# Output rows of a recurrent state-space layer with a mixture of experts: 32 indirect scatters from GpSimd in place of eight plain stores from SyncE

## The chip, the cores and the metric

The kernel runs on one core of one Trainium2 chip. The metric is the time of one execution on the device in microseconds (us). The core has five engines that run their own instruction streams and meet through semaphores: TensorE (PE in the profile, its weight loads PEld), VectorE (DVE), ScalarE (ACT), GpSimd (POOL) and SyncE (SP), which here only issues transfers. Sixteen DMA engines move the data between the memory of the chip and the on-chip tiles.

## The reference

The input x is 8 x 512 x 128 in float32: eight batches of 512 rows. With two branches s and g on the normalised rows, the output has x's shape and type:

```python
xn = _layernorm(x)
s = state_space(xn)        # conv over 3 rows, gates, a scan over the 512 rows of a batch, then
                           # ssm = ys @ D_w.T + D_b;  return ssm * gate
g = silu(mixture(xn))      # a dense gelu branch and 8 experts, 2 chosen per row
return x + s * g
```

In the scan each step is `s = layernorm(state @ A_bar + b_t)` and the row of y is `c_t * s`. Only the last line and the store of the result matter for the change.

## The kernel before

The 4096 rows (batch times 512) lie on the chip so that partition p holds the 32 consecutive rows 32p to 32p + 31: the tile X has the shape 128 partitions x 32 rows x 128 columns. NS = 32 is the number of such columns of rows, SUB = 4 how many of them make a group, NB = 8 the number of groups, L = 32 the rows of a partition. The kernel and this text call group n batch n; it holds rows 4n to 4n + 3 of each partition.

There are three blocks one after the other, with a barrier of all engines between them.

The first (up to about 100 us) loads the weights on SyncE (function load, L203) and x on ScalarE's queue, normalises, convolves and prepares weights. GpSimd's part begins with constants: memsets and masks (L244 to L265), the iota of 128x256 numbers into iota_i (L266) and its cast into rank (L268). After that GpSimd waits for the small weights (L274). VectorE uses rank when it chooses the experts (L776).

The second is the scan, in five rounds over 32 steps, with the eight experts of each group worked off beside it. It ends with the factor (silu of the mixture times the gate) of each group in the tile gi.

The third block, written out by hand engine by engine, makes the output, and it is what the change touches:

- VectorE normalises the states (L1373, four parts), TensorE transposes them (L1401, sixteen), ScalarE applies scale and bias (L1418), VectorE multiplies by C (L1379).
- TensorE makes ssm of a batch: a matmul of the bias over 512 columns (L1407) and eight products of 128x128 (L1409), in one of four banks.
- VectorE multiplies the bank by the factor and by 0.25 into outb, which is a view of the tile gi (L1383), and counts the semaphore gated_ssm.
- The residual x is added in place: by GpSimd for even batches (L1394, semaphore even_rows), by VectorE for odd ones (L1388, odd_rows).
- SyncE stores each batch, a transfer of 256 KB (L1426), as soon as even_rows or odd_rows says so, and waits at the end for all eight.

The store and the loop of GpSimd in two quotations:

```python
for n in range(NB):
    sp.wait_ge(sem("odd_rows" if n % 2 else "even_rows"), n // 2 + 1)
    sp.dma_start(rows_out[:, n * SUB:(n + 1) * SUB, :], outb[:, n]).then_inc(sem("out_stored"), 16)
```

Here rows_out is the output with the rows of a partition as its second axis, so that the four rows of a partition in one store are 2 KB in one piece.

Of the kernel before, what the change touches and what calls it, by code (L numbers as in the profile page):

```python
# [5 lines left out]
ALU = mybir.AluOpType  # L6
# [6 lines left out]
P = 128  # L13
# [19 lines left out]
def build(nc, I, out):  # L33
# [5 lines left out]
    SUB = T // P  # L39
# [5 lines left out]
    with ExitStack() as ctx:  # L45
        sems = {}

        def sem(name):
            if name not in sems:
                sems[name] = ctx.enter_context(nc.semaphore(name))  # L50
            return sems[name]

        def sb(name, shape, dt=F32):
            return ctx.enter_context(nc.sbuf_tensor(name, shape, dt))
# [9 lines left out]
        center = sb("center", [S, S])  # L64
        iota_i = sb("iota_i", [P, NS * E], mybir.dt.int32)
        rank = sb("rank", [P, NS, E])
        eps_col = sb("eps_col", [P, 1])
        junk_col = sb("junk_col", [P, 1])
        cols = sb("cols", [P, 24])
# [129 lines left out]
        with nc.Block() as front:  # L199
            @front.sync  # L200
            def _(sp):
                def load(dst, src, name="weights_loaded"):
                    sp.dma_start(dst, src).then_inc(sem(name), 16)  # L203

                def as_col(name):
                    return I[name].rearrange("(p a) -> p a", a=1)

                load(gens, I["L0_ffn_gens"].rearrange("m p n -> p m n"), "expm_loaded")
                load(A_in, I["L0_attn_A"], "expm_loaded")
                load(dt_row, I["L0_attn_dt_A"], "expm_loaded")  # L210
                load(gate_w[:, :, :], I["L0_attn_gate_w"].rearrange("(j p) h -> p j h", p=P), "matrices_loaded")
                load(BC_w[:, 0, :], I["L0_attn_B_w"], "matrices_loaded")
                load(BC_w[:, 1, :], I["L0_attn_C_w"], "matrices_loaded")
                load(D_w[:, 0, :], I["L0_attn_D_w"], "matrices_loaded")
                load(D_w[:, 1, :], I["L0_attn_D_w"], "matrices_loaded")
                load(ew2[:, :, :, :], I["L0_ffn_ew2"].rearrange("e (k p) d -> p e k d", p=P), "ew2_loaded")
                load(col["ln_in_g"], as_col("L0_attn_ln_in_g"))
                load(col["ln_in_b"], as_col("L0_attn_ln_in_b"))
                load(col["conv_b"], as_col("L0_attn_conv_b"))
                load(conv_w, I["L0_attn_conv_w"].rearrange("h a k -> h (a k)"))  # L220
                load(col["gate_b_in"], I["L0_attn_gate_b"][P:2 * P].rearrange("(p a) -> p a", a=1))
                load(col["ln_gamma"], as_col("L0_ffn_ln_gamma"))
                load(col["ln_beta"], as_col("L0_ffn_ln_beta"))
                load(col["B_b"][0:S], as_col("L0_attn_B_b"))
                for half in (slice(0, S), slice(S, P)):
                    load(col["ln_st_g"][half], as_col("L0_attn_ln_st_g"))
                    load(col["ln_st_b"][half], as_col("L0_attn_ln_st_b"))
                    load(C_b_col[half], as_col("L0_attn_C_b"))
                load(eb2[:, :], I["L0_ffn_eb2"])
                load(eb1_rows[:, :], I["L0_ffn_eb1"].rearrange("e (k p) -> (e k) p", p=P))  # L230
                load(gc_w_row, I["L0_ffn_gc_w"].rearrange("p a -> a p"))
                load(mgb_row, I["L0_ffn_moe_gate_b"].rearrange("(a p) -> a p", a=1))
                load(gc_b_row, I["L0_ffn_gc_b"].rearrange("(a p) -> a p", a=1))
                for i in range(3):
                    load(bias_in[i:i + 1, 0, :], I["L0_ffn_abel_b"].rearrange("(a p) -> a p", a=1), "biases_loaded")
                    load(bias_in[i:i + 1, 1, :], I["L0_attn_D_b"].rearrange("(a p) -> a p", a=1), "biases_loaded")
                    load(bias_in[i:i + 1, 2, :], I["L0_attn_gate_b"][0:P].rearrange("(a p) -> a p", a=1), "biases_loaded")
                load(abel_in[:, :], I["L0_ffn_abel_w"], "small_loaded")
                load(router_w[:, :], I["L0_ffn_moe_gate_w"], "small_loaded")
                load(ew1_in[:, :, :], I["L0_ffn_ew1"].rearrange("e d f -> d e f"), "ew1_loaded")  # L240

            @front.gpsimd
            def _(pool):
# [19 lines left out]
                pool.wait_ge(sem("shift2_ones"), 1)  # L263
                pool.memset(shift2[:, 0:P:SEG], 0.0)
                pool.memset(shift2[:, 1:P:SEG], 0.0)  # L265
                pool.iota(iota_i[:, :], pattern=[[0, NS], [-1, E]], base=E, channel_multiplier=0).then_inc(sem("iota_ready"), 1)  # L266
                pool.wait_ge(sem("iota_ready"), 1)
                pool.tensor_copy(rank[:, :, :], iota_i[:, :].rearrange("p (s e) -> p s e", s=NS)).then_inc(sem("rank_ready"), 1)  # L268
# [1096 lines left out]
        with nc.Block() as block:  # L1365
            @block.vector
            def _(dve):

                H2 = L // 4
                for g in range(4):  # L1370
                    part = slice(g * H2, (g + 1) * H2)
                    r = Rho[:, g * H2 + 1:(g + 1) * H2 + 1]
                    dve.tensor_tensor(Wst[:, part, :], Wst[:, part, :], r.unsqueeze(2).broadcast_to([P, H2, S]), ALU.mult).then_inc(sem("normalised"), 1)  # L1373

                for g in range(4):
                    part = slice(g * 4, (g + 1) * 4)
                    dve.wait_ge(sem("state_affine"), g + 1)
                    cs = csT[:, part, :].rearrange("p (b m) n -> p b m n", m=2)
                    dve.tensor_tensor(cs, cs, CT[:, 2 * g:2 * g + 2], ALU.mult).then_inc(sem("csT"), 1)  # L1379
                for n in range(NB):  # L1380

                    dve.wait_ge(sem("ssm"), n + 1)
                    dve.scalar_tensor_tensor(out=outb[:, n], in0=banks[4 + n % 4][:, :].rearrange("p (s h) -> p s h", s=SUB), scalar=0.25,  # L1383
                                             in1=factor[:, (n + 1) * SUB:(n + 2) * SUB, :], op0=ALU.mult, op1=ALU.mult).then_inc(sem("gated_ssm"), 1)

                    if n % 2:
                        dve.wait_ge(sem("gated_ssm"), n + 1)
                        dve.tensor_tensor(outb[:, n], outb[:, n], X[:, n * SUB:(n + 1) * SUB, :], ALU.add).then_inc(sem("odd_rows"), 1)  # L1388

            @block.gpsimd  # L1390
            def _(pool):
                for n in range(0, NB, 2):
                    pool.wait_ge(sem("gated_ssm"), n + 1)
                    pool.tensor_tensor(outb[:, n], outb[:, n], X[:, n * SUB:(n + 1) * SUB, :], ALU.add).then_inc(sem("even_rows"), 1)  # L1394

            @block.tensor
            def _(pe):
                for g in range(4):
                    pe.wait_ge(sem("normalised"), g + 1)
                    for q in range(4 * g, 4 * g + 4):  # L1400
                        t = pe.transpose(banks[g][:, (q % 4) * P:(q % 4 + 1) * P], Wst[:, 2 * q:2 * q + 2, :].rearrange("p k n -> p (k n)"), ident[:, :])  # L1401
                    t.then_inc(sem("cs_T"), 1)
                for n in range(NB):
                    pe.wait_ge(sem("csT"), n // 2 + 1)
                    if n >= 4:
                        pe.wait_ge(sem("gated_ssm"), n - 3)
                    pe.matmul(banks[4 + n % 4][:, :], ones3[:, :], D_b3, start=True, stop=False)  # L1407
                    for s in range(SUB):
                        t = pe.matmul(banks[4 + n % 4][:, s * P:(s + 1) * P], csT[:, 2 * n + s // 2, :], D_wT[:, s % 2, :],  # L1409
                                      start=False, stop=(s == SUB - 1))  # L1410
                    t.then_inc(sem("ssm"), 1)

            @block.scalar
            def _(act):
                for g in range(4):
                    act.wait_ge(sem("cs_T"), g + 1)

                    act.activation(csT[:, g * 4:g * 4 + 4, :], banks[g][:, :].rearrange("p (k n) -> p k n", k=4), ACT.Identity,  # L1418
                                   scale=col["ln_st_g"], bias=col["ln_st_b"]).then_inc(sem("state_affine"), 1)

            @block.sync
            def _(sp):
                rows_out = out.rearrange("b (q k) h -> (b q) k h", k=L)
                for n in range(NB):
                    sp.wait_ge(sem("odd_rows" if n % 2 else "even_rows"), n // 2 + 1)
                    sp.dma_start(rows_out[:, n * SUB:(n + 1) * SUB, :], outb[:, n]).then_inc(sem("out_stored"), 16)  # L1426
                sp.wait_ge(sem("out_stored"), 16 * NB)

# [26 lines left out]
```

## Time and profile before

| | us |
|---|---|
| timed runs (two) | 544.72 and 546.92 |
| their median | 545.82 |
| the profiled execution | 543.42 |
| its span, first to last instruction | 541.6 |
| TensorE busy in it | 444.0 (82%) |
| VectorE busy | 377.2 (70%) |
| ScalarE busy | 250.1 (46%) |
| GpSimd busy | 209.2 (39%) |

The profile is of one execution. Its span is 1.8 us shorter than that execution's own time, since it counts from the first to the last instruction. Starts are in us from the start of the span, durations of one instruction in us or ns as marked. Issues of transfers are not counted as busy time of the engine that issues them; they stand under its queue (SPq for SyncE).

### The profile page before, as it was taken

What the parts mean: (1) busy time and instruction counts of PE and PEld (TensorE: products, weight loads), DVE (VectorE), ACT (ScalarE), POOL (GpSimd) and SP (SyncE); (2) the same over time, 40 slices, a digit from 0 to 9 for tenths busy, and PEclk for the clock granted to TensorE, in tenths of its full rate; (3) what the DMA queues carried; (4) which work ended last, traced back from release to release, by engine and by line L of the source; (5) the groups of instructions that cost most, each with busy time, mean ns of one, the idle gap of its engine ahead of it and who ended that gap; (6) DMA issues with size and microseconds to landing.
All of it is one profiled execution on the core that took longest, in us unless ns stands there. A gap on an engine that the chain in (4) does not pass through costs nothing. (4 is left out here: it accounts for less than half of the span.)

```text
span 541.6 us, 13237 instructions
## 1 busy us (share of the span) xinstructions
PE 444.0 (82%) x4780; PEld 343.0 (63%) x4780; DVE 377.2 (70%) x1471; ACT 250.1 (46%) x597; POOL 209.2 (39%) x201
## 2 busy tenths in 40 slices
PE   2866799799889888988898898689889889998247
PEld 1766748477656666676676676567766566776135
DVE  3878579377878587777768676667677576868445
ACT  0325922445455335554455546154645355554420
POOL 2266645012532253243325414332443143425443
PEclk9959959899999798999999999799999799999759
DMA  8200000000000000000000000000000000000004
GB/s 268 79 7 0 2 1 1 2 1 2 2 2 2 1 2 1 1 2 1 2 2 0 3 1 1 2 1 2 1 2 2 1 1 2 2 1 2 0 4 155
DMA packets 6483, 7.65 MB, mean 14 GB/s; under 512 B 2424, under 2 KB 4378, under 8 KB 6426
## 3 DMA queue, kind: packets, MB, share of 16 engines
q1 hardware_dynamic: 5850, 4.77, 2.8%
q10 hardware_dynamic: 576, 2.10, 1.1%
q8 instruction: 39, 0.64, 0.5%
q14 instruction: 18, 0.15, 0.1%
HBM read 4.76 MB, written 2.10 MB: 13 GB/s over the span
## 5 line engine op out<-in xcount | busy, mean ns | idle before, releaser
L1336 POOL TENSOR_TENSOR xpad<-xpad 128x512 f32<-128x512 f32 x64 | 82.8, 1294 | 243.0 <-ACT xpad L1248 187.3
L1157 PE MATMUL bank<-ew,hT 128*128 128x128 f32 x1024 | 143.5, 289 | 0.0
L1248 ACT ACTIVATE xpad<-bank,wd 128x128 f32<-128x128 f32 x256 | 73.1, 369 | 128.4 <-PE bank L1157 128.2
L1157 PEld LDWEIGHTS bank<-ew,hT 128*128 128x128 f32 x1024 | 124.8, 195 | 9.1 <-issue 0.7
L1240 ACT ACTIVATE hT<-bank,eb_col 128x512 f32<-128x512 f32 x128 | 81.2, 687 | 50.7 <-PE bank L194 50.7
L980 PE MATMUL bank<-Mrep,wT 32*32 32x64 f32 x2560 | 69.7, 223 | 36.4 <-DVE wT L886 35.8
L980 PEld LDWEIGHTS bank<-Mrep,wT 32*32 32x32 f32 x2560 | 45.0, 106 | 77.8 <-issue 72.4
L896 DVE SCALAR_TENSOR_TENSOR ring<-bank,Rho,Dv 128x64 f32<-128x64 f32 x124 | 35.2, 284 | 65.1 <-PE bank L980 61.5
L192 PE MATMUL bank<-xf,ew_high 128*128 128x512 f32 x128 | 61.6, 481 | 0.0
L194 PE MATMUL bank<-xf,ew_rest 128*128 128x512 f32 x128 | 52.2, 408 | 0.0
L193 PE MATMUL bank<-xf,ew_high 128*128 128x512 f32 x128 | 52.2, 408 | 0.0
L852 DVE SCALAR_TENSOR_TENSOR roots<-z_all 128x1 f32<-128x1 f32 x96 | 34.0, 354 | 3.3
L886 DVE STREAM_TRANSPOSE wT<-ring 128x64 f32<-128x64 f32 x124 | 30.0, 242 | 2.0
L876 DVE CUSTOM_DVE_ANT_0 sqj<-ring,guess 128x64 f32<-128x64 f32 x64 | 30.4, 475 | 0.0
L192 PEld LDWEIGHTS bank<-xf,ew_high 128*128 128x128 f32 x128 | 25.1, 196 | 8.3 <-issue 0.9
L194 PEld LDWEIGHTS bank<-xf,ew_rest 128*128 128x128 f32 x128 | 25.2, 197 | 6.1
L857 DVE CUSTOM_DVE_ANT_0 sqj<-ring 128x64 f32<-128x64 f32 x64 | 27.2, 426 | 0.0
L193 PEld LDWEIGHTS bank<-xf,ew_high 128*128 128x128 f32 x128 | 25.4, 198 | 1.8
L896 DVE SCALAR_TENSOR_TENSOR late<-bank,Rho,Dv 128x64 f32<-128x64 f32 x31 | 8.8, 283 | 21.0 <-PE bank L980 20.3
L862 DVE SCALAR_TENSOR_TENSOR roots<-roots 128x1 f32<-128x1 f32 x64 | 21.6, 338 | 2.3
L626 DVE TENSOR_SCALAR zbuf<-X,lnv 128x128 f32<-128x128 f32 x32 | 18.8, 649 | 5.0 <-PE bank L340 5.0
L854 DVE SCALAR_TENSOR_TENSOR Rho<-roots,Rho 128x1 f32<-128x1 f32 x96 | 18.4, 192 | 3.3
(288 smaller groups left out, 716.5 us busy)
## 6 DMA issues: line engine op xcount, KB each, us to landing
X<-in_L_attn_x ACTq DMA_DIRECT2D x4, 512.0 KB, 6.1
out<-gi SPq DMA_DIRECT2D x8, 256.0 KB, 2.0
late<-in_L_ffn_ew SPq DMA_DIRECT2D x1, 1024.0 KB, 5.3
pulled<-in_L_ffn_gens SPq DMA_DIRECT2D x1, 192.0 KB
gate_w<-in_L_attn_gate_w SPq DMA_DIRECT2D x1, 128.0 KB, 7.4
D_w<-in_L_attn_D_w SPq DMA_DIRECT2D x2, 32.0 KB, 6.4
abel_in<-in_L_ffn_abel_w SPq DMA_DIRECT2D x1, 64.0 KB, 1.8
bias_in<-in_L_ffn_abel_b SPq DMA_DIRECT2D x3, 0.5 KB
```

The lines of the kernel that those rows point to most:

```text
L192: pe.matmul(o, a[0], b[0], start=start, stop=False)
L193: pe.matmul(o, a[0], b[1], start=False, stop=False)
L194: return pe.matmul(o, a[1], b[0], start=False, stop=stop)
L852: dve.scalar_tensor_tensor(out=w_now, in0=z, scalar=ROOT_LINEAR, in1=z, op0=ALU.add, op1=ALU.mult).then_inc(sem("root_w"), 1)
L876: dve.tensor_tensor_reduce(sqj[:, :], prev, prev, guess_scale[:, k:k + 1], guess_eps[:, k:k + 1], ALU.mult, ALU.add, z)\
L886: dve.transpose(wT[:, :], prev).then_inc(sem("state_T"), 1)
L896: dve.scalar_tensor_tensor(out=state(r, k), in0=psY, scalar=Rho[:, k:k + 1], in1=Dv[:, k, :], op0=ALU.mult, op1=ALU.add).then_inc(sem("sta ...
L980: t = pe.matmul(psY[q], wT[q, 32 * c:32 * c + 32], Mrep[q, c, :], start=(c == 0), stop=(c == 1))
L1157: t = pe.matmul(bE[e % 2][:, s * P:(s + 1) * P], hT[:, e % 2, k, s * P:(s + 1) * P], ew2[:, e, k, :], start=(k == 0), stop=(k == K - 1))
L1240: t = act.activation(hT[:, e % 2, k, :], bH[(e % 2) * 2 + k][:, :], ACT.Gelu, bias=eb1_col[:, e, k:k + 1])
L1248: t = act.activation(scaled[e % 2][:, s, :], bE[e % 2][:, s * P:(s + 1) * P], ACT.Copy, scale=w)
L1336: pool.tensor_tensor(acc, acc, scaled[e % 2], ALU.add).then_inc(sem("added"), 1)
```

## The change

The eight stores of SyncE are gone, and with them SyncE's part of the last block. GpSimd, between its adds, issues four indirect transfers for each batch. Each writes 128 rows of 512 bytes: the row of partition p goes to the row of the output whose number stands in row_ids[p, q], with q = 4n + s. The new tile row_ids is filled by an iota in the first block with q + 32p. GpSimd waits for all 32 at the end.

```diff
@@ -64,6 +64,7 @@
         center = sb("center", [S, S])
         iota_i = sb("iota_i", [P, NS * E], mybir.dt.int32)
         rank = sb("rank", [P, NS, E])
+        row_ids = sb("row_ids", [P, NS], mybir.dt.int32)
         eps_col = sb("eps_col", [P, 1])
         junk_col = sb("junk_col", [P, 1])
         cols = sb("cols", [P, 24])
@@ -263,6 +264,7 @@
                 pool.wait_ge(sem("shift2_ones"), 1)
                 pool.memset(shift2[:, 0:P:SEG], 0.0)
                 pool.memset(shift2[:, 1:P:SEG], 0.0)
+                pool.iota(row_ids[:, :], pattern=[[1, NS]], base=0, channel_multiplier=L).then_inc(sem("row_ids"), 1)
                 pool.iota(iota_i[:, :], pattern=[[0, NS], [-1, E]], base=E, channel_multiplier=0).then_inc(sem("iota_ready"), 1)
                 pool.wait_ge(sem("iota_ready"), 1)
                 pool.tensor_copy(rank[:, :, :], iota_i[:, :].rearrange("p (s e) -> p s e", s=NS)).then_inc(sem("rank_ready"), 1)
@@ -1389,9 +1391,18 @@
 
             @block.gpsimd
             def _(pool):
-                for n in range(0, NB, 2):
-                    pool.wait_ge(sem("gated_ssm"), n + 1)
-                    pool.tensor_tensor(outb[:, n], outb[:, n], X[:, n * SUB:(n + 1) * SUB, :], ALU.add).then_inc(sem("even_rows"), 1)
+                rows_out = out.rearrange("b t h -> (b t) h")
+                pool.wait_ge(sem("row_ids"), 1)
+                for n in range(NB):
+                    if n % 2 == 0:
+                        pool.wait_ge(sem("gated_ssm"), n + 1)
+                        pool.tensor_tensor(outb[:, n], outb[:, n], X[:, n * SUB:(n + 1) * SUB, :], ALU.add).then_inc(sem("even_rows"), 1)
+                    pool.wait_ge(sem("odd_rows" if n % 2 else "even_rows"), n // 2 + 1)
+                    for s in range(SUB):
+                        q = n * SUB + s
+                        pool.indirect_dma_start(rows_out, bass.IndirectOffsetOnAxis(ap=row_ids[:, q:q + 1], axis=0), outb[:, n, s, :], None)\
+                            .then_inc(sem("out_stored"), 16)
+                pool.wait_ge(sem("out_stored"), 16 * NS)
 
             @block.tensor
             def _(pe):
@@ -1418,14 +1429,6 @@
                     act.activation(csT[:, g * 4:g * 4 + 4, :], banks[g][:, :].rearrange("p (k n) -> p k n", k=4), ACT.Identity,
                                    scale=col["ln_st_g"], bias=col["ln_st_b"]).then_inc(sem("state_affine"), 1)
 
-            @block.sync
-            def _(sp):
-                rows_out = out.rearrange("b (q k) h -> (b q) k h", k=L)
-                for n in range(NB):
-                    sp.wait_ge(sem("odd_rows" if n % 2 else "even_rows"), n // 2 + 1)
-                    sp.dma_start(rows_out[:, n * SUB:(n + 1) * SUB, :], outb[:, n]).then_inc(sem("out_stored"), 16)
-                sp.wait_ge(sem("out_stored"), 16 * NB)
-
 
 # ---- launch: one core; inputs and outputs as the reference has them ----
 _INS = ["L0_attn_x", "L0_attn_A", "L0_attn_dt_A", "L0_attn_B_w", "L0_attn_B_b", "L0_attn_C_w", "L0_attn_C_b", "L0_attn_D_w",
```

On GpSimd, in the first block, before the change: the last mask, the iota of iota_i and the cast into rank (the tile shift2 goes as shift).

```order
L261 AFFINE_SELECT shift<-shift 128x128 [waits shift2_zero]
L264 MEMSET shift 128x8 [waits shift2_ones]
L265 MEMSET shift 128x8
L266 IOTA iota_i 128x256
L268 CAST rank<-iota_i 128x256 [waits iota_ready]
```

After it:

```order
L265 MEMSET shift 128x8 [waits shift2_ones]
L266 MEMSET shift 128x8
L267 IOTA row_ids 128x32
L268 IOTA iota_i 128x256
L270 CAST rank<-iota_i 128x256 [waits iota_ready]
L276 CAST abel_high<-abel_in 128x128 [waits small_loaded]
```

One iota has come in ahead of the other; everything behind it stands as before.

On GpSimd, at the end of the program, before the change (L1067 and L1068 close the second block, L1390 opens the third one, L1365 leaves it; gi is the tile of outb):

```order
L1055 COMPARE_AND_BRANCH
L1068 REGISTER_ALU
L1068 COMPARE_AND_BRANCH
L1067 UNCONDITIONAL_BRANCH
L1390 UNCONDITIONAL_BRANCH [waits barrier_Pool_Activation_PE_DVE_SP_gather]
L1394 TENSOR_TENSOR gi<-gi,X 128x512 [waits gated_ssm] x4
L1365 UNCONDITIONAL_BRANCH
```

After it, from the branch into the third block up to the end of batch 4's first scatter:

```order
L1392 UNCONDITIONAL_BRANCH [waits barrier_Pool_Activation_PE_DVE_SP_gather]
L1399 TENSOR_TENSOR gi<-gi,X 128x512 [waits gated_ssm,row_ids]
L1403 DMA out<-gi,row_ids 4096x128 [waits even_rows]
L1403 DMA out<-gi,row_ids 4096x128 x3
L1403 DMA out<-gi,row_ids 4096x128 [waits odd_rows]
L1403 DMA out<-gi,row_ids 4096x128 x3
L1399 TENSOR_TENSOR gi<-gi,X 128x512 [waits gated_ssm]
L1403 DMA out<-gi,row_ids 4096x128 [waits even_rows]
L1403 DMA out<-gi,row_ids 4096x128 x3
L1403 DMA out<-gi,row_ids 4096x128 [waits odd_rows]
L1403 DMA out<-gi,row_ids 4096x128 x3
L1399 TENSOR_TENSOR gi<-gi,X 128x512 [waits gated_ssm]
```

The four adds stood one behind the other, each waiting only for VectorE. Now eight scatters stand between one add and the next, four for the even batch and four for the odd one, and the order goes on in this way up to batch 7.

On SyncE, the end of the program before the change:

```order
L203 DMA late<-in_L_ffn_ew 128x8x256
L199 UNCONDITIONAL_BRANCH
L1421 UNCONDITIONAL_BRANCH [waits barrier_Pool_Activation_PE_DVE_SP_release]
L1426 DMA out<-gi 128x512 [waits even_rows]
L1426 DMA out<-gi 128x512 [waits odd_rows]
L1426 DMA out<-gi 128x512 [waits even_rows]
L1426 DMA out<-gi 128x512 [waits odd_rows]
L1426 DMA out<-gi 128x512 [waits even_rows]
L1426 DMA out<-gi 128x512 [waits odd_rows]
L1426 DMA out<-gi 128x512 [waits even_rows]
L1426 DMA out<-gi 128x512 [waits odd_rows]
L1365 UNCONDITIONAL_BRANCH [waits out_stored]
```

After it:

```order
L204 DMA bias_in<-in_L_attn_gate_b 1x128
L204 DMA abel_in<-in_L_ffn_abel_w 128x128
L204 DMA router_w<-in_L_ffn_moe_gate_w 128x8
L204 DMA late<-in_L_ffn_ew 128x8x256
L200 UNCONDITIONAL_BRANCH
```

SyncE has nothing left behind the loads of the first block.

## Rows read from the trace of the kernel before

**Rows 1.** The chain of waits that ended last: start us, us, what.

```profile
522.17 3.68 PE bank L1401 x16
...
536.26 0.32 PE bank L1407
536.58 1.10 PE bank L1409 x8
...
537.70 0.70 DVE gi L1383
...
538.43 0.69 DVE gi L1388
```

**Rows 2.** The timeline from 515 us on: start us, us, engine, line, operation.

```profile
517.12 1.26 POOL L1128 TENSOR_TENSOR xpad<-xpad 128x512 f32<-128x512 f32 x1
518.46 1.26 POOL L1133 TENSOR_TENSOR xpad<-xpad 128x512 f32<-128x512 f32 x1
...
528.63 1.27 POOL L1394 TENSOR_TENSOR gi<-gi,X 128x512 f32<-128x512 f32 x1 [7.58 <-DVE gi L1383]
...
529.27 0.69 DVE L1383 SCALAR_TENSOR_TENSOR gi<-bank,gi 128x512 f32<-128x512 f32 x1 [0.71 <-PE bank L1409]
...
529.93 9.55 SPq L1426 DMA_DIRECT2D out<-gi  x8
...
531.45 1.26 POOL L1394 TENSOR_TENSOR gi<-gi,X 128x512 f32<-128x512 f32 x1 [1.54 <-DVE gi L1383]
```

**Rows 3.** The line of the stores, L1426: ns min/median/max, and time to landing.

```profile
L1426 SPq DMA_DIRECT2D out<-gi x8: 332/332/358, 529.9 to 539.1; - x8
...
DMA to landing us min/median/max: 2.0/2.0/2.1
```

**Rows 4.** The timeline of GpSimd at the start.

```profile
3.38 0.11 POOL L265 MEMSET shift<- 128x8 f32 x1
3.43 0.44 POOL L266 IOTA iota_i<- 128x256 int32 x1
3.94 0.40 POOL L268 CAST rank<-iota_i 128x256 f32<-128x256 int32 x1
23.97 0.30 POOL L274 CAST abel_high<-abel_in 128x128 fp32r<-128x128 f32 x1 [19.63 <-DMA router_w<-in_L_ffn_moe_gate_w]
```

**Rows 5.** The instructions that write or read the tile rank.

```profile
L268 POOL CAST rank<-iota_i x1: 397/397/397, 3.9 to 3.9; 128x256 f32<-128x256 int32 x1
L776 DVE TENSOR_TENSOR scratch<-scratch,rank x1: 500/500/500, 88.4 to 88.4; 128x256 f32<-128x256 f32 x1
```

**Rows 6.** Two kinds of GpSimd operation, by line: L301, and the adds L1394.

```profile
L301 POOL TENSOR_TENSOR bias_rest<-bias_rest,bias_part x1: 905/905/905, 26.9 to 26.9; 3x384 f32<-3x384 f32 x1
...
L1394 POOL TENSOR_TENSOR gi<-gi,X x4: 1264/1266/1269, 528.6 to 537.1; 128x512 f32<-128x512 f32 x4
```

**Rows 7.** The DMA queues in the stretch 529.9 to 541.6 us.

```profile
DMA packets 1152, 2.10 MB, mean 179 GB/s; under 512 B 128, under 2 KB 128, under 8 KB 1152
...
q1 hardware_dynamic: 1152, 2.10, 47.0%
```

**Rows 8.** Busy time by engine in the stretch 529.9 to 541.6 us.

```profile
core 0: us, PE busy (x) PEld busy (x) DVE busy (x) ACT busy (x) POOL busy (x), PEclk, DMA share, GB/s
529.90:541.60 11.70, 7.76 (x52) 5.84 (x50) 6.94 (x11) 0.00 (x0) 3.80 (x4) 0.96 0.47 179
```

## The prediction

> **What bounds the kernel now.** I read the chain that ended last first [rows 1]. Up to 537.7 us, for 15.5 us, it is TensorE: sixteen transposes at L1401, then for each of the eight batches one bias matmul (L1407, 0.32 us) and eight matmuls (L1409, 1.09 us), a beat of 1.41 us. The last batch leaves through two VectorE operations, L1383 and L1388, and is ready at 538.43 + 0.69 = 539.12 us. What the chain does not count is the last store. The timeline of the stretch and the line of the stores give it [rows 2, 3]: SyncE issues the first store at 529.93, just as GpSimd's add of batch 0 ends (528.63 + 1.27 = 529.90), and the eighth at 539.1; a store lands 2.0 to 2.1 us after its issue, so about 541.2, and the span ends at 541.6, another 0.4 later. The stores are hidden in the beat: one issue takes 332 ns of SyncE, eight of them 2.7 us in 9.3 us. Everything before 528 us I need only for the new iota.
>
> **What the change moves.** Every store leaves SyncE and every row goes out in a scatter of 128 rows, one from each partition, 512 B a row; four scatters a batch, 32 in all, all issued by GpSimd, which also keeps its four adds. The order of GpSimd's instructions has them as one queue: add, 4 scatters, 4 scatters, add, and so on. So two things that ran on two engines now run on one, one after the other, and an even batch's add waits behind the eight scatters before it even where its data is ready.
>
> Removed: eight issues on SyncE, 8 x 0.33 us, all beside TensorE's beat except the last. That last one (0.33 us) is inside the 2.1 us to landing [rows 3]; nothing else goes.
>
> Added at the start: one iota of 128x32 on GpSimd, ahead of the iota of 128x256 that takes 0.44 us, the small memset beside it 0.11 us [rows 4]. It costs 0.1 to 0.4 us, and delays the cast into rank by as much. Nobody is hurt: GpSimd then sits idle for 19.63 us until a weight lands [rows 4], and rank, ready at 4.3 us, is read at 88.4 us at first [rows 5]. I count 0. Without that idle time it would be at most 0.4 us. The wait for the semaphore row_ids in the last block was met 520 us earlier: 0.
>
> Added at the end: 32 scatters. No row of this kernel shows GpSimd issue any transfer, so the price c of one (the time until GpSimd can start the next) is bounded from both sides. Low end: 0.33 us, SyncE's issue of a store that also names 128 pieces [rows 3]. High end: 2.1 us, the time from issue to landing [rows 3], if each scatter had to be through before the next can begin. Between them lie GpSimd's own operations: 0.905 us for 3x384 elements and 1.27 us for 128x512 [rows 6]. A scatter makes a program on GpSimd read 128 row numbers and make 128 reads and 128 writes of them, one after another; that is work like that of these two rows, and far more than a queued instruction. I take the middle of the two, 1.1 us, the nearest rows on the engine that does the work.
>
> **The sum.** The first scatter can start where the first store did, 529.9. From there GpSimd has 32c, and three more adds at 1.27 us with the 0.07 us that lie between one GpSimd operation and the next (starts at 517.12 and 518.46, 1.34 apart, for a duration of 1.26 [rows 2]): 3 x 1.34 = 4.0 us. The start of the second one now (531.45 [rows 2]) is only the earliest possible, since the queue reaches it later. After the last scatter is issued its rows must land: 2.1 - 0.33 = 1.8 us. Then 0.4 us to the end of the span. End = 529.9 + 32c + 4.0 + 1.8 + 0.4 = 536.1 + 32c, against 541.6: the change costs 32c - 5.5 us. With c = 1.1 it is 35.2 - 5.5 = 29.7 us. The profiled execution took 543.4 us, so it would take 573.1; the median of the two timed runs is 545.8, 2.4 above it, and on that base the forecast is 575.5 us. TensorE and VectorE don't feel it: no buffer of theirs is given back by a store (VectorE overwrites no row that is being stored), and both are done at 539.1 as before.
>
> Do the DMA engines set a slower pace than GpSimd? The eight stores are 1152 packets (1024 of 2 KB, 128 small) that hold the 16 engines for 47.0% of 11.7 us [rows 7]: 88 us, 76 ns a packet. A scatter is 128 packets of 512 B plus 16 small ones, 9 per engine; at 76 ns that is 0.69 us, under the 1.1 us, and an upper bound, since a quarter of the bytes should not take as long. So the price is GpSimd's, and 0.69 us is a floor only in the case of cheap issues: 32 x 0.69 - 5.5 = 16.6 us.
>
> Beside this there is VectorE. From 529.90 to the end it is busy 6.94 us [rows 8]. If GpSimd could write no transfer while VectorE works, that is at most 6.9 us more. The rows speak against it: L1394 takes 1264 to 1269 ns in all four instances, the first of them half beside L1383 [rows 6, 2]. I count 0, and keep 6.9 for the top of the range.
>
> The Trainium skill, page "SBUF — State Buffer", warns of just this: a DMA issued from GpSimd starves of descriptors while VectorE holds the port pair that the two share. By it the four L1388 operations, with both inputs in SBUF, could cost up to their own length here, an estimate of 2.8 us by the 0.69 us of their row; no run here shows a scatter beside them yet.
>
> **Rivals.**
> A, issuing is cheap (the ending that is not slower). GpSimd hands a scatter over as quickly as SyncE hands a store, and the work is done behind its back. Place: the queue after 529.9. Price: c = 0.33 gives 10.6 - 5.5 = 5.1 us, 550.9 us, within 2%. The point from which it decides is the price at which 32c - 5.5 is 2%, 10.9 us: c = 0.51. Against a real gain speaks that batch 7 is ready at 539.12 whatever the stores do: only with c under some 0.17 would the end come no later than now. For it speaks the 332 ns row, in which the issue of 128 pieces costs no more than a small one; against it that this is another generator, and that even then the DMA engines may hold it to 0.69 us.
>
> The page "DMA: Bandwidth & Descriptors", section on the anatomy of one DMA, of the Trainium skill, leans to A: many descriptors can be emitted before their number begins to cost, and most of the fixed 2.0 us is the receipt of the write. The trace agrees with the 2.0 us (2.0 to 2.1), and shows nothing on the other point. The same page gives about 1 us to the first byte from GpSimd; taken as the price of each scatter it would make, as an estimate, 32 x 1.0 - 5.5 = 26.5 us, 572.3 us.
>
> B, one at a time. If a scatter holds GpSimd, or its ring, until the one before has landed, c is about 2.1: 67.2 - 5.5 = 61.7 us, 607.5 us. For it: all 32 come from one engine, count on one semaphore and read their row numbers from one tile. Against: the code waits only once, at the end, and SyncE's stores don't wait for each other.
>
> C, the DMA engines decide: c = 0.69, 562.4 us, as worked out above. It needs a GpSimd faster than its own smallest full operations in [rows 6] and packets as slow as those of 2 KB.
>
> D, it doesn't do what it says: the scatters split a row of 128 floats into smaller pieces. Then the count of packets is far above 32 x 144 = 4608, and the end goes out beyond B's. Nothing in the program hints at it; a row is contiguous on both sides.
>
> **How the numbers follow.** The forecast (c from 0.8 to 1.6, 565.9 to 591.5 us) has 0.72; A 0.06; C and what lies between it and A, 0.09; B and what lies between 1.6 and 2.1, 0.11; D 0.02. A measurement of this kernel tells 2%, 10.9 us, from no change. Slower by more than that is everything from c = 0.51 on: 0.93. Within it is A: 0.06. Faster needs a kernel that ends before its own last batch is stored: 0.01. The range reaches down into C and the upper part of A's neighbourhood, to c = 0.56 (558 us), and up to c = 1.86 (600 us), which holds the 6.9 us of VectorE on top of the forecast and part of the way to B. The predicted time is rounded to 575.5.
>
> **What would show it.** In the profile after: GpSimd's queue with 32 issues from 529.9 without a gap but for three adds, the last at about 568; the mean distance of two scatters in a batch is c; the span's last waits are on GpSimd's queue, not on VectorE; TensorE and VectorE done at 539.1; 4608 packets in a queue of its own. The forecast is wrong if c is under 0.5 (then A, with the adds following within a few us of their old starts), if the distance equals the time to landing (B), or if the scatters are issued fast and the DMA engines are busy all the time up to the end (C). A time that moves in the part before 520 us would mean that something else than the stores has changed.

## The result, and the profile after

The changed kernel takes 581.88 us (median of 580.41 and 583.34) against 545.82: a ratio of 1.070 with a 95% interval of 1.055 to 1.085, slower by 36 us. In a second comparison it took 583.09 against 544.43, a ratio of 1.071 (1.061 to 1.080).

The page of the profile after, its lines of busy time, of the queues and of the scatters (line, engine, operation, count, busy us and mean ns, then idle time just before):

```profile
span 581.5 us, 13263 instructions
...
PE 443.9 (76%) x4780; PEld 343.3 (59%) x4780; DVE 378.2 (65%) x1471; ACT 250.0 (43%) x597; POOL 241.4 (42%) x234
...
q1 hardware_dynamic: 4698, 2.67, 1.8%
q0 software_dynamic: 1024, 2.10, 1.1%
...
L1403 POOL DMA_INDIRECT out<-gi,row_ids x32 | 31.9, 996 | 9.7 <-issue 8.5
```

The span is 581.5 us, 39.9 longer than before. TensorE's busy time has not moved (444.0 before), nor VectorE's to speak of (377.2 before, 378.2 now). Queue q0 has taken the 2.10 MB that q1 had [rows 7], in packets of two kinds, as the count from 525 us on shows: for each scatter 16 of 4 KB, each with eight rows of 512 bytes, and 16 small ones.

```profile
DMA packets 1025, 2.11 MB, mean 37 GB/s; under 512 B 512, under 2 KB 512, under 8 KB 1024
```

The scatters' line (ns min/median/max of one):

```profile
L1403 POOL DMA_INDIRECT out<-gi,row_ids x32: 955/959/1462, 532.0 to 576.2; - x32
...
  issue: 8.5, 28
  POOL gi L1399: 1.1, 4
```

The timeline of the last block after, to be laid beside [rows 2] (start, us, engine, line, operation):

```profile
530.43 1.27 POOL L1399 TENSOR_TENSOR gi<-gi,X 128x512 f32<-128x512 f32 x1 [7.62 <-DVE gi L1385]
...
531.72 0.69 DVE L1390 TENSOR_TENSOR gi<-gi,X 128x512 f32<-128x512 f32 x1
532.00 1.46 POOL L1403 DMA_INDIRECT out<-gi,row_ids  x1 [0.29 <-POOL gi L1399]
...
533.76 0.96 POOL L1403 DMA_INDIRECT out<-gi,row_ids  x1 [0.30 <-issue]
533.81 0.69 DVE L1385 SCALAR_TENSOR_TENSOR gi<-bank,gi 128x512 f32<-128x512 f32 x1 [0.71 <-PE bank L1420]
...
534.53 0.69 DVE L1390 TENSOR_TENSOR gi<-gi,X 128x512 f32<-128x512 f32 x1
535.02 1.03 POOL L1403 DMA_INDIRECT out<-gi,row_ids  x1 [0.30 <-issue]
...
536.36 0.96 POOL L1403 DMA_INDIRECT out<-gi,row_ids  x1 [0.30 <-issue]
...
537.35 0.69 DVE L1390 TENSOR_TENSOR gi<-gi,X 128x512 f32<-128x512 f32 x1
537.63 1.24 POOL L1403 DMA_INDIRECT out<-gi,row_ids  x1 [0.30 <-issue]
...
539.18 0.96 POOL L1403 DMA_INDIRECT out<-gi,row_ids  x1 [0.31 <-issue]
...
540.16 0.69 DVE L1390 TENSOR_TENSOR gi<-gi,X 128x512 f32<-128x512 f32 x1
540.44 1.24 POOL L1403 DMA_INDIRECT out<-gi,row_ids  x1 [0.30 <-issue]
541.98 0.96 POOL L1403 DMA_INDIRECT out<-gi,row_ids  x1 [0.30 <-issue]
542.96 1.28 POOL L1399 TENSOR_TENSOR gi<-gi,X 128x512 f32<-128x512 f32 x1
...
544.51 0.98 POOL L1403 DMA_INDIRECT out<-gi,row_ids  x1 [0.28 <-POOL gi L1399]
...
574.91 0.96 POOL L1403 DMA_INDIRECT out<-gi,row_ids  x1 [0.31 <-issue]
576.18 0.96 POOL L1403 DMA_INDIRECT out<-gi,row_ids  x1 [0.30 <-issue]
```

Read it from the top. The add of batch 0 ends at 531.70 and the first scatter starts 0.30 later. From then on GpSimd does nothing but scatters and three adds. A scatter holds it 0.96 us, and 0.30 us pass before the next begins: the distance is 1.264 us (the last two start 1.27 apart). An add between two scatters puts 1.27 us on top. VectorE's last operation, L1390 at 540.16, ends at 540.85, 35 us before GpSimd's last scatter begins, at 576.18. The span ends 5.3 us after that start.

The last block begins at different times in different profiles (VectorE's first operation there, over Rho, at 521.42 us before and 523.17 after), so I compare from that start to the end of the span: 20.18 us before, 58.33 us after, 58.43 us in a second profile of the changed kernel. The change costs 38.15 us there, and the other 1.75 us lie ahead of the block.

### The profile page after: what moved, and what is told of

Same layout as the page of the kernel before. It is cut to its first block and busy times, and to the rows that moved or that the text cites. A ratio compares the mean times of both kernels' runs of the same rounds, so it can differ in the third digit from the quotient of the medians.

```text
span 581.5 us, 13263 instructions
## 1 busy us (share of the span) xinstructions
PE 443.9 (76%) x4780; PEld 343.3 (59%) x4780; DVE 378.2 (65%) x1471; ACT 250.0 (43%) x597; POOL 241.4 (42%) x234
## 3 DMA queue, kind: packets, MB, share of 16 engines
q0 software_dynamic: 1024, 2.10, 1.1%
## 5 line engine op out<-in xcount | busy, mean ns | idle before, releaser
L1403 POOL DMA_INDIRECT out<-gi,row_ids x32 | 31.9, 996 | 9.7 <-issue 8.5
L864 DVE SCALAR_TENSOR_TENSOR roots<-roots 128x1 f32<-128x1 f32 x64 | 21.6, 337 | 2.3
L898 DVE SCALAR_TENSOR_TENSOR late<-bank,Rho,Dv 128x64 f32<-128x64 f32 x31 | 8.8, 283 | 21.0 <-PE bank L982 20.2
```

The lines of the kernel that those rows point to most:

```text
L898: dve.scalar_tensor_tensor(out=state(r, k), in0=psY, scalar=Rho[:, k:k + 1], in1=Dv[:, k, :], op0=ALU.mult, op1=ALU.add).then_inc(sem("sta ...
L1403: pool.indirect_dma_start(rows_out, bass.IndirectOffsetOnAxis(ap=row_ids[:, q:q + 1], axis=0), outb[:, n, s, :], None)\
```

## The experiments

All numbers "last block" are from VectorE's first operation there to the end of the span, in one profile each: 20.2 us before, 58.3 us after. It is far steadier than the whole time: its start lay between 515.5 and 523.3 us in the profiles of all kernels but early32 (531.75). In the quotations of edits, indentation, the counting of semaphores behind a transfer (`.then_inc`) and changes of the final wait that follow from the number of transfers are left out; `...` stands for lines between.

| kernel | stores | last block, us | ratio to before (interval) |
|---|---|---|---|
| before | 8 from SyncE | 20.18 | 1 |
| sp_plain32 | 32 from SyncE | 25.23 | 1.013 (1.004 to 1.022) |
| gp_plain8 | 8 plain from GpSimd | 21.60 | 1.005 (1.001 to 1.009) |
| gp_plain32 | 32 plain from GpSimd | 35.22 | 1.025 (1.017 to 1.033) |
| scatter8_2k | 8 scatters | 26.56 | 1.015 (1.006 to 1.024) |
| half_half | 16 scatters, 4 from SyncE | 36.41 | 1.026 (1.015 to 1.036) |
| after_again | 32 scatters | 58.43 | 1.071 (1.061 to 1.080) |
| rows64 | 32 scatters of 64 rows | 56.48 | 1.067 (1.059 to 1.075) |
| rows16 | 32 scatters of 16 rows | 55.27 | one run, no ratio |
| late_start | 32 scatters, later | 67.58 | one run, no ratio |
| one_by_one | 32 scatters, each waited for | 97.95 | one run, no ratio |
| iota_only | 8 from SyncE, and the iota | 20.25 | 1.000 (0.996 to 1.004) |
| early32 | 8 from SyncE, 32 small GpSimd loads early | 20.15 | 1.018 (1.008 to 1.028) |

**Who issues, and how many: sp_plain32.**

```diff
-    sp.dma_start(rows_out[:, n * SUB:(n + 1) * SUB, :], outb[:, n])
+    for s in range(SUB):
+        q = n * SUB + s
+        sp.dma_start(rows_out[:, q, :], outb[:, n, s, :])
```

> The kernel before with each store cut into four, 32 plain transfers of 128 x 512 bytes from SyncE. Theory (the price is that of GpSimd making the transfer): SyncE issues one in 0.33 us, four in 1.33 us, under the beat of 1.41 us, so only the last batch adds three issues, 1.0 us; 547 us, same. Rival (32 small transfers cost wherever they come from, 1.26 us apart): about 580 us.

The count alone costs 5.0 us, not 1.0. Its timeline and the line of the stores show why my number was off: an issue with pieces of 512 bytes takes 432 ns, not the 332 of pieces of 2 KB [rows 3], and SyncE needs 15.08 us for 32, 0.47 us each. Four are 1.9 us, over the beat of 1.41 us, so that SyncE falls behind TensorE.

```profile
531.51 15.08 SPq L1428 DMA_DIRECT2D out<-gi  x32
```

```profile
L1428 SPq DMA_DIRECT2D out<-gi x32: 358/432/439, 531.5 to 546.1; - x32
...
DMA to landing us min/median/max: 1.6/1.7/1.7
```

Of the 38 us that is 5. The other 33 come with the move to GpSimd.

**Generator or indices: gp_plain32.**

```diff
-    rows_out = out.rearrange("b t h -> (b t) h")
+    rows_plain = out.rearrange("b (q k) h -> (b q) k h", k=L)
...
-    pool.indirect_dma_start(rows_out, bass.IndirectOffsetOnAxis(ap=row_ids[:, q:q + 1], axis=0), outb[:, n, s, :], None)
+    pool.dma_start(rows_plain[:, q, :], outb[:, n, s, :])
```

> The changed kernel with its 32 scatters as plain transfers of the same rows, from GpSimd; nothing reads row_ids. Theory A (GpSimd's program for 128 pieces costs 1.26 us whatever names the rows): distance of two transfers 1.26 us, about 581 us. Rival B (the indices are the price): distance 0.5 us or less, under 560 us.

Theory A falls. The timeline shows the same queue, with eight transfers in 4.26 us, and the line of the transfers 537 ns for one:

```profile
533.70 1.28 POOL L1399 TENSOR_TENSOR gi<-gi,X 128x512 f32<-128x512 f32 x1
535.27 4.26 POOL L1403 DMA_DIRECT2D out<-gi  x8 [0.29 <-POOL gi L1399]
```

```profile
L1403 POOL DMA_DIRECT2D out<-gi x32: 537/537/718, 529.2 to 550.7; - x32
...
DMA to landing us min/median/max: 1.8/1.8/2.2
```

They stand back to back, with no 0.30 us between them. A plain transfer of 128 pieces costs GpSimd 0.533 us, the indirect one 1.264: 0.73 us of a scatter, 58% of it, is what the indirect form costs over the plain one. With 23.1 us of 38 it is the largest part of the loss (58.33 - 35.22); 10.0 us are the plain transfers' move from SyncE to GpSimd (35.22 - 25.23).

**Bytes: scatter8_2k and gp_plain8.** One scatter a batch, each of 128 numbers and 128 pieces of 2 KB; and one plain transfer a batch.

```diff
-    pool.iota(row_ids[:, :], pattern=[[1, NS]], base=0, channel_multiplier=L)
+    pool.iota(row_ids[:, :], pattern=[[1, NS]], base=0, channel_multiplier=NB)
...
-    rows_out = out.rearrange("b t h -> (b t) h")
+    rows_out = out.rearrange("b (t k) h -> (b t) (k h)", k=SUB)
...
-    for s in range(SUB):
-        q = n * SUB + s
-        pool.indirect_dma_start(rows_out, bass.IndirectOffsetOnAxis(ap=row_ids[:, q:q + 1], axis=0), outb[:, n, s, :], None)
+    pool.indirect_dma_start(rows_out, bass.IndirectOffsetOnAxis(ap=row_ids[:, n:n + 1], axis=0), gi[:, n, :], None)
```

> Scatters of 128 pieces of 2 KB, one per batch, eight in place of 32. Theory (price per scatter or per row number, not per byte): eight at 1.26 us, about 551 us, +1% on before. Rival (price per byte): four times 1.26 us each, about 580 us.

```diff
-    rows_out = out.rearrange("b t h -> (b t) h")
+    rows_plain = out.rearrange("b (q k) h -> (b q) k h", k=L)
...
-    for s in range(SUB):
-        q = n * SUB + s
-        pool.indirect_dma_start(rows_out, bass.IndirectOffsetOnAxis(ap=row_ids[:, q:q + 1], axis=0), outb[:, n, s, :], None)
+    pool.dma_start(rows_plain[:, n * SUB:(n + 1) * SUB, :], outb[:, n])
```

> The changed kernel with one plain transfer of 256 KB per batch from GpSimd, eight in all. If a transfer costs 1.26 us there: GpSimd has 4 adds and 8 transfers, 15.2 us from 528.6 on, so its last issue ends at about 544 and the time is about 551 us (+1%). If the price goes with bytes (5 us each): about 585 us.

Four times the bytes cost GpSimd next to nothing: the lines of the transfers show 0.96 us again as the shortest scatter, and 0.55 us for a plain transfer. (The median of the scatters, 972 ns, lies higher because three of the eight begin beside one of VectorE's adds, which is taken up under late_start.)

```profile
L1401 POOL DMA_INDIRECT out<-gi,row_ids x8: 960/972/1469, 531.4 to 545.2; - x8
```

```profile
L1401 POOL DMA_DIRECT2D out<-gi x8: 539/551/720, 526.7 to 535.8; - x8
...
DMA to landing us min/median/max: 2.3/2.5/2.6
```

The price is one per instruction. Eight scatters leave 6.4 us of the 38.

**Rows: rows64 and rows16.** Both leave output rows unwritten, as their expectations say; rows16 has 16 where this diff has 64.

```diff
-    pool.indirect_dma_start(rows_out, bass.IndirectOffsetOnAxis(ap=row_ids[:, q:q + 1], axis=0), outb[:, n, s, :], None)
+    pool.indirect_dma_start(rows_out, bass.IndirectOffsetOnAxis(ap=row_ids[0:64, q:q + 1], axis=0), outb[0:64, n, s, :], None)
```

> The changed kernel with 32 scatters of the first 64 partitions alone; half of the output is not written. If the 1.26 us is all per row: 0.63 us, about 562 us. If all fixed: 1.26 us, about 581 us. Between them the split into a fixed part and a part per row is read from the distance of two scatters.

> The changed kernel with 32 scatters of the first 16 partitions alone; seven eighths of the output are not written. 128 rows gave 0.959 us, 64 gave 0.895: if the price is linear, 0.83 + 0.001 x 16 = 0.85 us and a distance of 1.15 us; if there is a step in it, less than 0.8 us.

```profile
L1403 POOL DMA_INDIRECT out<-gi,row_ids x32: 888/895/1357, 526.5 to 569.0; - x32
```

```profile
L1403 POOL DMA_INDIRECT out<-gi,row_ids x32: 845/849/1358, 531.8 to 573.2; - x32
```

959, 895 and 849 ns for 128, 64 and 16 rows: from 128 to 64 rows 1.0 ns a row, from 64 to 16 also 1.0. The line through them meets no rows at 0.83 us. With the 0.30 us between two scatters, 1.13 us of the 1.264 is fixed and 0.13 us depends on the rows. Of the two ends of my expectation for rows64 it lies all but at "all fixed".

**The slow ones among the first eight: late_start.**

Ahead of GpSimd's loop over the batches:

```diff
+    pool.wait_ge(sem("gated_ssm"), NB)
+    pool.wait_ge(sem("odd_rows"), NB // 2)
```

> The changed kernel with GpSimd waiting until VectorE has finished its last operation before it adds or scatters anything. Theory (VectorE's work beside them is what made four of the first eight scatters take 1.03 to 1.46 us): all eight take 0.96 us. Rival (the first scatters are slow by themselves, a start-up): the same four are slow again. The time grows by the 9 us of waiting less 1.1 us in the first case, to about 590 us.

Its timeline has GpSimd's first three scatters:

```profile
532.89 1.26 POOL L1401 TENSOR_TENSOR gi<-gi,X 128x512 f32<-128x512 f32 x1 [17.72 <-DVEq L1367]
534.44 1.17 POOL L1405 DMA_INDIRECT out<-gi,row_ids  x1 [0.29 <-POOL gi L1401]
535.91 0.96 POOL L1405 DMA_INDIRECT out<-gi,row_ids  x1 [0.30 <-issue]
537.18 0.96 POOL L1405 DMA_INDIRECT out<-gi,row_ids  x1 [0.30 <-issue]
```

Both theories hold in part. The first scatter is slow by itself (1.17 us, 0.21 above the others); the 3rd, 5th and 7th are not slow when VectorE is done. The timeline of the changed kernel says what they wait for. Their starts (535.02, 537.63, 540.44) all fall into an L1390, VectorE's add with both inputs in SBUF, and what they lose is what is left of it, less a constant 0.13: L1390 ends at 535.22, 538.04 and 540.85, that is 0.20, 0.41 and 0.41 after the starts, and the scatters are 0.07, 0.28 and 0.28 longer than 0.96. The first one has 0.41 of an L1390 left too, and loses 0.29 beyond its 0.21. The scatters that start beside an L1385 instead, with one input from a bank (533.76 beside 533.81), take 0.96. Together 0.92 us by L1390 and 0.21 by the first one. The same sum comes out in rows16, where a scatter alone takes 0.85: the one at 540.07 finds 0.63 us of an L1390 left and is 0.50 longer, again 0.13 less.

```profile
540.01 0.69 DVE L1390 TENSOR_TENSOR gi<-gi,X 128x512 f32<-128x512 f32 x1
540.07 1.35 POOL L1403 DMA_INDIRECT out<-gi,row_ids  x1 [0.30 <-issue]
```

In gp_plain32 only one of 32 is above 537 ns by much (718, the maximum above, again 0.18 more); early32, whose transfers run elsewhere, has the same pair of 537 and 717. In gp_plain32 the second group of eight (535.27 to 539.53) begins while an L1390 runs (534.58 to 535.54), and another falls right into it:

```profile
534.58 0.96 DVE L1390 TENSOR_TENSOR gi<-gi,X 128x512 f32<-128x512 f32 x1
...
537.39 0.69 DVE L1390 TENSOR_TENSOR gi<-gi,X 128x512 f32<-128x512 f32 x1
```

That group takes 4.26 us like those after VectorE's end. So the plain transfers don't lose anything to L1390.

The Trainium skill, page "SBUF — State Buffer", section "Who interferes with whom", says that a VectorE operation with two SBUF inputs holds off a GpSimd instruction that reads SBUF, and not one that only writes it. The trace agrees: the scatter, which reads its row numbers, loses 0.92 us, and the plain transfer loses nothing. That it is the reading of the row numbers, and not another part of the indirect form, no run here takes apart.

The adds of the two engines, with two SBUF inputs each, also meet where GpSimd is less far behind, and there it is VectorE that loses. In scatter8_2k an L1390 takes 2.05 us in place of 0.69 beside a GpSimd add that begins 0.22 us after it (in half_half 1.84); in the changed kernel they never meet.

```profile
533.90 2.05 DVE L1390 TENSOR_TENSOR gi<-gi,X 128x512 f32<-128x512 f32 x1
534.12 1.27 POOL L1399 TENSOR_TENSOR gi<-gi,X 128x512 f32<-128x512 f32 x1
```

**Rival B: one_by_one.**

Behind each scatter:

```diff
+    pool.wait_ge(sem("out_stored"), 16 * (q + 1))
```

> The changed kernel with GpSimd waiting for each scatter to land before the next. The distance of two scatters is then the time from start to landing. If the late end (4.4 us from the last scatter's end to the end of the span) is the landing of a scatter, the distance is over 4 us and the time over 670 us. If a scatter lands about as fast as a store (2.1 us after its start, so about 1.2 us after its end), the distance is 2.1 to 2.6 us, the time 610 to 625 us, and the late end is something at the end of the program.

```profile
612.76 0.96 POOL L1403 DMA_INDIRECT out<-gi,row_ids  x1 [1.56 <-DMA out<-gi,row_ids]
615.28 0.96 POOL L1403 DMA_INDIRECT out<-gi,row_ids  x1 [1.56 <-DMA out<-gi,row_ids]
```

The distance is 2.52 us, double that of the changed kernel. So scatters do overlap with the landing of those before, and rival B is wrong. And a scatter has landed at most 2.5 us after its start, yet the span ends 5.4 us after the last start (620.7 - 615.28). The profile of after_again gives the landing itself:

```profile
DMA to landing us min/median/max: 2.2/2.3/3.2
```

**The late end: half_half and early32.** The first, on the changed kernel, leaves GpSimd the even batches and gives SyncE the odd ones.

```diff
-    pool.wait_ge(sem("odd_rows" if n % 2 else "even_rows"), n // 2 + 1)
-    for s in range(SUB):
...
+    if n % 2 == 0:
+        pool.wait_ge(sem("even_rows"), n // 2 + 1)
+        for s in range(SUB):
...
+    for n in range(1, NB, 2):
+        sp.wait_ge(sem("odd_rows"), n // 2 + 1)
+        sp.dma_start(rows_plain[:, n * SUB:(n + 1) * SUB, :], outb[:, n])
```

> The even batches by 16 scatters from GpSimd, the odd ones by four plain stores from SyncE. Theory (the queue of GpSimd decides): from the first add 4 x (1.27 + 0.30) + 16 x 1.264 us and the end, so the last block is about 17 us longer than in the kernel before in place of 38. The end of the span comes about 1.7 us after the last scatter has landed if that rest grows by 0.083 us with each transfer of GpSimd (1.1 us with 8, 3.1 us with 32); 3.1 us if it is a fixed price of the changed block.

The second is the kernel before, with loads from GpSimd in the first block, behind its cast into rank.

```diff
+    for i in range(NS):
+        pool.dma_start(unused[:, i:i + 1], I["L0_ffn_ln_gamma"].rearrange("(p a) -> p a", a=1))
```

> The kernel before, plus 32 small plain loads from GpSimd into a tile that nothing uses, issued in the first block while GpSimd is idle; stores as before, from SyncE. If the rest at the end comes from the number of transfers that GpSimd has issued in the whole program: 2.7 us longer at the end, 3.1 us from the landing of the last store to the end of the span in place of 0.4. If it comes from transfers issued shortly before the end: 0.4 us as before.

From the landing of the last transfer (last start plus the median time to landing) to the end of the span: before 0.4 us; sp_plain32 0.4 (546.1 + 1.7 to 548.2); gp_plain8 1.1 (535.8 + 2.5 to 539.4); half_half 1.75, from the rows below and 553.7; gp_plain32 3.1 (550.7 + 1.8 to 555.6); after_again 3.1 (576.3 + 2.3 to 581.7); one_by_one 3.1 (615.28 + 2.3 to 620.7). It grows with the number of transfers that GpSimd issues in the last block, by 0.08 us each, plain or indirect, waited for one by one or not. 32 transfers of GpSimd in the first block leave 0.5 (549.4 + 2.0 to 551.9), so that those of an earlier block don't count at the end.

```profile
L1404 POOL DMA_INDIRECT out<-gi,row_ids x16: 957/962/1463, 526.1 to 549.7; - x16
L1439 SPq DMA_DIRECT2D out<-gi x4: 332/338/358, 526.5 to 535.2; - x4
...
DMA to landing us min/median/max: 2.0/2.3/2.9
```

What the time is spent on stays open: no row of the profile lies in it.

early32 is slower by 1.8% for another reason, which the row of the first use of the small weights shows (at 23.97 us in [rows 4]):

```profile
4.53 17.08 POOL L273 DMA_DIRECT2D unused<-in_L_ffn_ln_gamma  x32
37.15 0.30 POOL L278 CAST abel_high<-abel_in 128x128 fp32r<-128x128 f32 x1 [15.54 <-DMA router_w<-in_L_ffn_moe_gate_w]
```

The early transfers hold GpSimd from 4.53 to 21.6 us, in its idle time as meant, but the loads of SyncE land 13 us later beside them, and the last block begins at 531.75 us, 10.3 later than in the kernel before. Each of these transfers is 0.5 KB in pieces of 4 bytes, one a partition, so they are not an image of the stores. That the one delays the other is read from the two rows; what they share was not taken apart.

**The start: after_again and iota_only.** The changed kernel without an edit, and the kernel before with this one:

```diff
+    row_ids = sb("row_ids", [P, NS], mybir.dt.int32)
+    pool.iota(row_ids[:, :], pattern=[[1, NS]], base=0, channel_multiplier=L)
```

> The changed kernel once more, beside the others on one chip. From the first normalising operation of VectorE in the last block (the line multiplying by Rho) to the end of the span it took 58.3 us, 20.2 us in the kernel before. Theory: 58.3 us again, within 0.3, and a ratio of about 1.07; the start of the last block may lie some us elsewhere.

> The kernel before with the new tile and its iota alone. Theory: within 0.3% of before, and the 1.75 us by which the last block began later in the changed kernel are the scatter of runs. Rival: the iota or the tile's place costs them, 547.5 us, +0.3%.

The iota and the tile cost nothing that can be told, to 0.4%. Its last block began at 516.95, 4.5 us earlier than that of the kernel before in its profile, and the changed kernel's at 523.17 and 523.27. The 1.75 us ahead of the block are thus within what profiles of such kernels differ by. They aren't shown to be anything else.

None of these kernels is faster than the kernel before, and none points to one that would be: the nearest, gp_plain8, is 0.5% behind.

## Why the prediction was right, and where it was not

575.5 us were forecast, in a range of 558 to 600; 581.9 were measured. Of the 38.15 us in the last block 29.7 were forecast. (The profiled execution, 583.34 us against 573.1 forecast for it, has the 1.75 us ahead of the block on top; the medians differ by 6.4.) Where the other 8.4 are:

| term | forecast, us | measured, us |
|---|---|---|
| 31 distances of scatters | 34.1 | 39.2 (1.264 each) |
| wait beside VectorE, and the first scatter | 0 | 1.1 |
| gap ahead of the first scatter | 0 | 0.3 |
| three adds | 4.0 | 3.9 |
| from the last scatter's start to the end | 3.3 | 5.3 |

- **What bounds it.** Right. All ends in GpSimd's queue, adds and scatters one after the other, and VectorE and TensorE end as early as before: VectorE 17.7 us after the start of the block in both.
- **The price c.** The mis-sized term. "I take the middle of the two, 1.1 us": it is 1.264, and 5.1 of the 8.4 us come from here. The reason given for it was wrong beyond its size: "a program on GpSimd read 128 row numbers and make 128 reads and 128 writes of them, one after another". A row costs 1.0 ns, 0.13 us for all. 1.13 us of the 1.264 is paid for the instruction, and 0.30 of that between two of them, where the profile shows GpSimd neither busy nor waiting for anything. The rows of GpSimd's operations on tiles were near in size by chance: an operation whose time goes with its elements says nothing of one whose price is nearly all fixed. That the time fell into the range is due to this luck as much as to the queue, which was read rightly.
- **Rival B** would be a distance of 2.52 us as built in one_by_one, 622.5 us; I had put it at 607.5. It isn't what happens.
- **Rival C.** Queue q0 holds 1.1% of 16 engines' span (581.5 us), 102 us in all, for 32 scatters 0.2 us on each engine. My bound of 0.69 was loose: eight rows leave together as one packet of 4 KB.
- **Rival D** as I named it (packets far above 4608) is excluded, and my own count too: 1024 packets. 4608 is what SyncE makes of the same rows, in sp_plain32.
- **VectorE.** "The rows speak against it ... I count 0." It costs 0.92 us, by L1390 alone. My row was the wrong witness: L1394 stood beside L1383, which has one input in a bank, and never beside the add with two inputs in SBUF. The estimate of 2.8 us was an upper bound of the right kind: each scatter lost only what was left of an L1390 when it began. But the reason given beside it doesn't fit. The Trainium skill, page "SBUF — State Buffer", section "SBUF: two separate sides", states the starving of descriptors for VectorE's two-port modes, and it would strike plain transfers of GpSimd too; gp_plain32's lost nothing beside an L1390.
- **The start.** Right: iota_only shows nothing, with an interval of 0.4% to either side. The iota took 0.15 us and pushed rank's cast from 3.94 to 4.19 us.
- **The end.** "2.1 - 0.33 = 1.8 us. Then 0.4 us" is short by 2.0 us. With c it puts the landing 2.9 us after the last start, and it came after 2.3, 0.6 earlier; the rest at the end, taken as fixed, grows with GpSimd's transfers from 0.4 to 3.1 us, 2.7 more. The two errors partly cancel.

## What to carry to other kernels

Moving a store to GpSimd as an indirect transfer costs 1.26 us of that engine each for 128 rows, 1.15 for 16, and no more with 2 KB a row than with 512 bytes: so make each scatter carry as much as it can (2 KB a row in place of 512 bytes took 32 us of 38 away), and use a plain transfer where the rows are known when the program is built. Before you move issues to an engine, lay their sum beside the beat of the stage: 0.33 us on SyncE vanished in 1.41 us a batch, while 4 x 1.26 us could not. Where no row shows an operation's price, ask separately for what it costs per instruction and per element, since a similar size of a neighbour says nothing of how it will scale.

## What the runs showed that I had not expected

- The 0.30 us after each scatter, in which GpSimd starts nothing; plain transfers from the same engine stand back to back.
- A scatter that begins beside one of VectorE's adds with two SBUF inputs waits for it, all but 0.13 us; a plain transfer does not.
- Where the adds of GpSimd and VectorE meet, VectorE's takes up to 2.05 us in place of 0.69.
- The end of the span comes 0.08 us later for each transfer that GpSimd issued in the last block, though all have landed.
- SyncE's issue depends on the pieces: 332 ns for 128 of 2 KB, 432 ns for 128 of 512 bytes.
- Beside 32 loads of GpSimd, 512 bytes each in pieces of 4, SyncE's weights came 13 us later at the start.
